# A selective scan with both directions' decay factors made in one instruction, one group ahead, and the matrix engine's queue reordered

## What is computed

```
dA  = exp(-delta[..., None] * exp(A_log))
dBu = delta[..., None] * Bm[:, :, None, :] * xc[..., None]
h   = dA * h + dBu          # for the five tokens in turn, h starts at 0
y   = einsum("bdn,bn->bd", h, c)
```

## Time and profile before

| | |
|---|---|
| Time, median of 3 runs | 537.95 us (536.87 to 539.11) |
| Time of the profiled execution | 537.0 us |
| Its span in the profile | 535.2 us |
| TensorE busy (matmul) | 484.4 us, 91% |
| VectorE busy | 380.0 us, 71% |
| ScalarE busy | 237.7 us, 44% |
| GpSimd busy | 171.3 us, 32% |
| The scan: first `argument` to last `outputs` | from 310.55 to 465.19 us of the span |

### The profile page before, as it was taken

How to read it: one execution, slowest core, us unless ns; L and a number is a source line. 1 busy time by engine, 2 the same in 40 slices (tenths; PEclk the granted TensorE clock), 3 DMA queues, 4 the chain that set the end, 5 groups by cost and what they waited for, 6 DMA issues and landing times. The chain is left out here.

```text
span 535.2 us, 6853 instructions
## 1 busy us (share of the span) xinstructions
PE 484.4 (91%) x1812; PEld 237.1 (44%) x1812; DVE 380.0 (71%) x718; ACT 237.7 (44%) x416; POOL 171.3 (32%) x163
## 2 busy tenths in 40 slices
PE   6989999999999998996879568989999998989997
PEld 3545555555555465543546312222222222376653
DVE  0066576575566677653999759999999999287655
ACT  1112213212222311659969537788878888121100
POOL 6000100100100112222250016888888888242000
PEclk9999999999999999999588959999999999999999
DMA  9981009300000000500334765665557565400000
GB/s 267 308 263 41 1 5 318 97 1 1 1 1 0 0 1 1 149 0 0 104 103 131 213 185 146 163 193 149 165 148 202 144 169 158 118 4 12 10 11 20
DMA packets 36426, 53.55 MB, mean 100 GB/s; under 512 B 5652, under 2 KB 27184, under 8 KB 36402
## 3 DMA queue, kind: packets, MB, share of 16 engines
q1 hardware_dynamic: 35746, 52.52, 34.3%
q10 hardware_dynamic: 656, 0.73, 0.4%
HBM read 35.83 MB, written 17.27 MB: 99 GB/s over the span
## 5 line engine op out<-in xcount | busy, mean ns | idle before, releaser
L1686 POOL TENSOR_TENSOR gb<-da,hb 128x512 f32<-128x512 f32 x94 | 117.1, 1281 | 65.8 <-ACT da L1622 65.8
L1716 DVE TENSOR_TENSOR da<-ps,expA 128x512 f32<-128x512 f32 x128 | 84.9, 683 | 10.1 <-PE ps L1520 8.9
L304 PE MATMUL ps<-xbuf,convw 128*128 128x384 f32 (+1 forms) x240 | 82.9, 499 | 4.8 <-DMA convw<-in_conv_wT 4.8
L1622 ACT ACTIVATE da<-da 128x512 f32<-128x512 f32 x128 | 78.0, 626 | 17.0 <-DVE da L1716 14.7
L358 PE MATMUL ps<-wall,peT 128*128 128x512 f32 x144 | 67.8, 593 | 0.0
L1520 PE MATMUL ps<-drows,selb 96*128 96x512 bf16 x128 | 50.5, 400 | 16.3 <-DMA drows<-dparts 10.5
L304 PEld LDWEIGHTS ps<-xbuf,convw 128*128 128x128 f32 (+1 forms) x240 | 46.0, 194 | 36.7 <-ACTq L501 4.0
L1532 PE MATMUL ps<-urows,brows 96*128 96x512 bf16 x128 | 48.8, 399 | 1.4 <-DVE gb L1723 0.8
L528 ACT ACTIVATE kvs<-ps 128x512 f32<-128x512 f32 x36 | 21.5, 597 | 57.4 <-PE ps L358 57.4
L520 ACT ACTIVATE peT<-ps 128x384 f32<-128x384 f32 x24 | 11.8, 491 | 75.4 <-PE ps L304 75.4
L1734 DVE TENSOR_TENSOR hb<-gb,ps 128x512 f32<-128x512 f32 x64 | 42.0, 676 | 0.0
(11 more groups left out here) (218 smaller groups left out, 746.4 us busy)
## 6 DMA issues: line engine op xcount, KB each, us to landing
xbuf<-in_xT SPq DMA_DIRECT2D x11, 768.0 KB
yscr<-yst SPq DMA_DIRECT2D x30, 208.0 KB
brows<-bparts SPq DMA_DIRECT2D x16, 240.0 KB, 3.3
uparts<-pt SPq DMA_DIRECT2D x24, 128.0 KB, 2.4
dparts<-pt SPq DMA_DIRECT2D x24, 128.0 KB, 2.4
drows<-dparts SPq DMA_DIRECT2D x15, 192.0 KB, 2.7
urows<-uparts SPq DMA_DIRECT2D x15, 192.0 KB, 3.2
inw<-in_in_wT SPq DMA_DIRECT2D x2, 1024.0 KB
```

The source lines that it names most:

```text
L304: mm = pe.matmul(bank(T_EMB + j % 2, 0, EN), convw[0:n, k, h * P:(h + 1) * P], xbuf[0:n, q, k, c * EN:(c + 1) * EN], start=(k == 0), stop= ...
L1622: act.activation(da_at(q, j), da_at(q, j), ACT.Exp, scale=-1.0).then_inc(da_ready, 1)
L1686: pool.tensor_tensor(gb_at(q, j), da_at(q, j), hb[:, s_ - 2, d, :], ALU.mult).then_inc({2: m2_done, 3: m3_done, 4: m4_done}[s_], 1)
L1716: dve.tensor_tensor(da_at(q, j), bank(j % 2), expA[:, j % 2, :], ALU.mult).then_inc(e_free, 1)
```

## The change

- `argument` and `exponential` become `arguments(g, q, s_)` and `exponentials(g, q, s_)`: one instruction of 128x1024 for both directions, four a group in place of eight of 128x512. `spread_delta` becomes `spread_pair`: two matmuls into banks 0 and 1, released together, and both banks are freed together.
- All four steps of group g+1 are made in the body of group g ("one group ahead"), and `spread_pair` of step 0 for group g+2 too. A new buffer `da1` holds steps 1 and 2 of odd groups.
- On TensorE, `spread_pair(g+1, 1)` stands ahead of `add_decayed(g-1, 1)` and `spread_pair(g+2, 0)` ahead of `add_decayed(g, 0)`.
- At the scan's start, VectorE makes the first decayed state and the first states of group 0 before it waits for the arguments of steps 2 and 3, whose rows arrive late. TensorE asks for the rows of group 1 before the first body.
- SyncE loads the delta rows of group g+2 at once, and the u and B rows behind the store of y.
- The expert weights `expw` move into the space of `inw`, which is no longer used by then, to make room for `da1`.

The number of matmuls, of states and of GpSimd instructions stays.

```diff
-        expw = sb("expw", [P, CH, E8 * C])
+        expw = inw[:, :, :, :].rearrange("p d h n -> p d (h n)")
+        da1 = sb("da1", [P, 4, DI], ctx=scn)
...
-        def da_at(q, j):
-            return da[:, j + (2 if j >= 6 and q == 1 else 0), :]
+        def da_at(q, j, n=1):
+            if j >= 2 and q == 1:
+                return da1[:, j - 2:j - 2 + n, :] if j < 6 else da[:, j + 2:j + 2 + n, :]
+            return da[:, j:j + n, :]
...
 # SyncE, body of group g
-                        sp.wait_ge(e_ready, 8 * g + 8)
-                        load_rows(sp, g + 2, q)
+                        sp.wait_ge(e_ready, 4 * g + 4)
+                        load_delta(sp, g + 2, q, 0, ST)
                     if last and q == 1:
                         last_y(0)
                     else:
                         store_y(g, 0)
+                    if not last:
+                        load_u(sp, g + 2, q, 0, ST)
+                        load_b(sp, g + 2, q)
...
 # TensorE
-            def spread_delta(g, q, j):
-                o = (j // 2) * DI
-                pe.wait_ge(e_free, 8 * g + j + 1)
-                pe.matmul(bank(j % 2), selb[:, j % 2, :], drows[:, q, o:o + DI],
-                          start=True, stop=True).then_inc(e_ready, 1)
+            def spread_pair(g, q, s_):
+                pe.wait_ge(e_free, 4 * g + s_ + 1)
+                for d in range(2):
+                    mm = pe.matmul(bank(d), selb[:, d, :], drows[:, q, s_ * DI:(s_ + 1) * DI], start=True, stop=True)
+                mm.then_inc(e_ready, 1)
...
             pe.wait_ge(d_landed[0], 16 * 2)
-            for j in range(4, 6):
-                spread_delta(0, 0, j)
+            spread_pair(0, 0, 2)
+            spread_pair(0, 0, 3)
+            pe.wait_ge(d_landed[1], 16)
+            spread_pair(1, 1, 0)
...
                     b_times_u(g, q, 4)
+                    b_times_u(g, q, 5)
+                    if after:
+                        spread_pair(g + 1, 1 - q, 1)
                     if not (first and q == 0):
                         add_decayed(g - 1, 1 - q, 1)
-                    b_times_u(g, q, 5)
-                    spread_delta(g, q, 6)
...
                     b_times_u(g, q, 6)
                     b_times_u(g, q, 7)
-                    spread_delta(g, q, 7)
                     if after:
-                        pe.wait_ge(d_landed[1 - q], 16 * (i + q) + (16 if q == 0 else 32))
-                        spread_delta(g + 1, 1 - q, 0)
+                        spread_pair(g + 1, 1 - q, 2)
                     outputs(g, q, 0)
...
                         b_times_u(g + 1, 1 - q, 0)
-                        spread_delta(g + 1, 1 - q, 1)
                         b_times_u(g + 1, 1 - q, 1)
-                        spread_delta(g + 1, 1 - q, 2)
-                        spread_delta(g + 1, 1 - q, 3)
+                        spread_pair(g + 1, 1 - q, 3)
                     if not (first and q == 0):
                         outputs(g - 1, 1 - q, 1)
                     if after:
-                        spread_delta(g + 1, 1 - q, 4)
                         b_times_u(g + 1, 1 - q, 2)
                         b_times_u(g + 1, 1 - q, 3)
+                    if not last:
+                        pe.wait_ge(d_landed[q], 16 * i + (48 if q == 0 else 32))
+                        spread_pair(g + 2, q, 0)
                     add_decayed(g, q, 0)
-                    if after:
-                        spread_delta(g + 1, 1 - q, 5)
...
 # ScalarE, body of group g
                         copy_state(g - 1, 1)
-                    exponential(g, q, 4)
-                    exponential(g, q, 5)
+                    if after:
+                        exponentials(g + 1, 1 - q, 0)
                     stage_c(g, q)
-                    exponential(g, q, 6)
-                    exponential(g, q, 7)
+                    if after:
+                        exponentials(g + 1, 1 - q, 1)
                     copy_y(g, 0)
...
 # VectorE
-            for j in range(3):
-                argument(0, 0, j)
-            decayed_1(0, 0, 0)
-            decayed_1(0, 0, 1)
-            argument(0, 0, 3)
+            for s_ in range(2):
+                arguments(0, 0, s_)
+            for d in range(2):
+                decayed_1(0, 0, d)
             for d in range(2):
                 state(0, 0, 1, d)
+            for s_ in range(2, 4):
+                arguments(0, 0, s_)
...
-                    argument(g, q, 4)
-                    argument(g, q, 5)
-                    argument(g, q, 6)
+                    if after:
+                        arguments(g + 1, 1 - q, 0)
                     state(g, q, 2, 0)
-                    argument(g, q, 7)
+                    if after:
+                        arguments(g + 1, 1 - q, 1)
                     state(g, q, 2, 1)
                     if after:
-                        for j in range(3):
-                            argument(g + 1, 1 - q, j)
-                        for d in range(2):
-                            decayed_1(g + 1, 1 - q, d)
-                        argument(g + 1, 1 - q, 3)
+                        arguments(g + 1, 1 - q, 2)
+                        decayed_1(g + 1, 1 - q, 0)
+                        decayed_1(g + 1, 1 - q, 1)
+                        arguments(g + 1, 1 - q, 3)
                         for d in range(2):
                             state(g + 1, 1 - q, 1, d)
```

More of the change, by code:

```diff
@@ L1242, in prepare_vector @@
             ch = Chain(dve, x_chain)
-            dve.sem_inc(e_free, 2)
+            dve.sem_inc(e_free, 1)
             dve.sem_inc(bu_used, 2)
@@ L1560, in scan_tensor @@
             pe.wait_ge(skip_ready, NI - 1)
-            for j in range(4):
-                spread_delta(0, 0, j)
+            for s_ in range(2):
+                spread_pair(0, 0, s_)
             pe.wait_ge(u_landed[0], 16 * 4)
@@ L1613, in scan_tensor @@
             pe.wait_ge(w_landed, W_ALL)
-            pe.wait_ge(e_free, 2 + 8 * NG)
+            pe.wait_ge(e_free, 1 + 4 * NG)
             keep_clock(6)
@@ L1619, in scan_scalar, with exponentials @@
         def scan_scalar(act):
-            def exponential(g, q, j):
-                act.wait_ge(e_free, 2 + 8 * g + j + 1)
-                act.activation(da_at(q, j), da_at(q, j), ACT.Exp, scale=-1.0).then_inc(da_ready, 1)
+            def exponentials(g, q, s_):
+                act.wait_ge(e_free, 1 + 4 * g + s_ + 1)
+                act.activation(da_at(q, 2 * s_, 2), da_at(q, 2 * s_, 2), ACT.Exp, scale=-1.0).then_inc(da_ready, 1)
             def copy_y(g, k):
@@ L1638, in copy_state @@
                 act.activation(hb[:, 2, d, :], bank(4 + d), ACT.Copy).then_inc(h3_copied, 1)
-            for j in range(4):
-                exponential(0, 0, j)
+            for s_ in range(4):
+                exponentials(0, 0, s_)
             def body(i, first, last):
@@ L1648, in body @@
                         copy_state(g - 1, 1)
-                    exponential(g, q, 4)
-                    exponential(g, q, 5)
+                    if after:
+                        exponentials(g + 1, 1 - q, 0)
                     stage_c(g, q)
-                    exponential(g, q, 6)
-                    exponential(g, q, 7)
+                    if after:
+                        exponentials(g + 1, 1 - q, 1)
                     copy_y(g, 0)
                     if after:
-                        for j in range(3):
-                            exponential(g + 1, 1 - q, j)
+                        exponentials(g + 1, 1 - q, 2)
+                        exponentials(g + 1, 1 - q, 3)
                     if not (first and q == 0):
@@ L1660, in body @@
                     if after:
-                        exponential(g + 1, 1 - q, 3)
                         copy_state(g, 0)
@@ L1674, in decayed @@
                 j = 2 * (s_ - 1) + d
-                pool.wait_ge(da_ready, 8 * g + j + 1)
+                pool.wait_ge(da_ready, 4 * g + s_)
                 if s_ == 4:
@@ L1685, in decayed @@
                     need(pool, y_done[1], g)
-                pool.tensor_tensor(gb_at(q, j), da_at(q, j), hb[:, s_ - 2, d, :],
+                pool.tensor_tensor(gb_at(q, j), da_at(q, j)[:, 0, :], hb[:, s_ - 2, d, :],
                                    ALU.mult).then_inc({2: m2_done, 3: m3_done, 4: m4_done}[s_], 1)
@@ L1706, in scan_vector, with arguments @@
             dve.wait_ge(skip_ready, NI)
-            def argument(g, q, j):
-                dve.wait_ge(e_ready, 8 * g + j + 1)
-                if j in (2, 3):
-                    need(dve, m2_done, 2 * g + j - 3)
-                elif j in (4, 5):
-                    need(dve, m3_done, 2 * g + j - 5)
-                elif j >= 6:
-                    need(dve, m4_done, 2 * g + j - 9)
-                dve.tensor_tensor(da_at(q, j), bank(j % 2), expA[:, j % 2, :], ALU.mult).then_inc(e_free, 1)
+            def arguments(g, q, s_):
+                dve.wait_ge(e_ready, 4 * g + s_ + 1)
+                if s_ == 0:
```

(11 more changed lines are left out.)

10 lines of the change are left out of this document (2 added, 8 removed).

## The result

The changed kernel takes 559.12 us (median of 4 runs, 558.02 to 561.70) against 537.78 us for the kernel before (4 runs): ratio 1.039, 95% interval 1.035 to 1.044. The forecast was 556.6 (543 to 566). The profiled execution has 558.86 us and a span of 557.1.

What follows compares the result with a forecast made beforehand. The prediction took VectorE as the bound in the scan of the kernel before. To the profiled 537.0 us it added 14.0 for the scan periods and 5.6 for the start, giving 556.6 us, range 543 to 566.

Steps and rivals of the forecast that it cites:

- The chain: Scan loop: waits through in-order queues from arguments to the next make periods 9.80 us, straight ones 9.58; +14.0 us, chance 0.63.
- The bound of +15.6 for a signal of 0.2: Scan periods: upper limit if the queue waits add up as summed, with 0.2 us for releasing TensorE; +15.6 us.
- The merging, 0.07 us a pair: VectorE arguments: one 1024-wide instruction starts its follower after 1.13 us against 1.20 for two; 0.28 us gained a group.
- The start: Scan start: late rows, both-bank hand-over and low TensorE clock delay group 1's first state; +5.6 us, +3.6 if the clock rises.
- The end: After group 15's first state: GpSimd's 7.45 us of work covers the arguments VectorE no longer has; 0 us.
- The DMA order: u and B rows, issued behind the store of y, land at 12.0 and are read at 15.6: hidden, 3 us to spare.
- The VectorE-bound case: Scan, faster rival: add_decayed and copy_state delay nothing, group takes 8.12 us, -9.1 us, total 531.5 us; chance 0.08.
- The period of 9.08 for bank waits only: Scan rival: outputs does not wait for stage_c, only waits before arguments 1 and 2 remain; +4.3 us, 545 to 546.5; chance 0.12.
- The clock did not fall in the loop: Scan rival: TensorE's clock falls inside the scan, +4.4 us a group affected, 565 for two, 579 for five; chance 0.11.

Runs made afterwards that it cites:

- Two edits that each cut one link: Changed kernel with add_decayed(g-1, 1) back ahead of the spreads of step 1: 548.7 us; or with stage_c ahead of the exponential: 551.2 us; both together: 550.5 us.
- the additions at the head in both kernels: Changed kernel with both add_decayed moved ahead of the spreads on TensorE: 537.7 us with 512-wide arguments, 544.9 us with 1024-wide ones.
- split kernels: Changed kernel with arguments 512 wide again, each bank filled and freed by itself: 550.8 us; with both add_decayed also ahead of the spreads: 537.7 us.
- the kernel with split arguments and early additions: Changed kernel with 512-wide arguments, single spreads and both add_decayed ahead of the spreads on TensorE: 537.7 us, ratio 0.999.
- the kernel with the addition back: Changed kernel with add_decayed(g-1, 1) back between the two b_times_u, ahead of the spreads of step 1: 548.7 us, ratio 1.020.

## Why the prediction was right

- **The chain, +14.0 forecast, +13.6 measured.** The links, forecast and measured from 376.15 on: arguments to spreads 1.31 and 1.28; spreads 0.43 and 0.44; addition to `copy_state` 1.06 and 1.06; `copy_state` to exponential 0.50 and 0.49; exponential to `stage_c` 0.95 and 0.95; `stage_c` to `outputs` 0.58 and 0.45 (0.59 in the other group of the pair); `outputs` to `b_times_u` 0.98 and 0.98; to `decayed_1` 0.51 and 0.42; and the rest of VectorE's queue 3.53 and 3.53. Two edits that each cut one link took 8.0 and 7.5 us away, and together 8.3: both links lie on one chain, shown. That the sum agrees to 0.4 us is in part luck: the 12 loop periods were 9.67 on average where 9.80 was forecast, 1.5 us less in all, and the two straight ones 10.67 and 9.61 in place of 9.58, 1.1 more, since the first of them still ran at the low clock. The bound of +15.6 for a signal of 0.2 should be +15.4 to +16.1 by the same terms.
- **The merging, 0.07 us a pair.** The row of SBUF to SBUF held for PSUM too: 1.13 to 1.14 from start to start, 1.22 long. The formula of the Trainium skill (VectorE: DVE Perf Modes, the section on the TRN2 errata) gives 1.224 us for the length, and the measured 1.22 agrees. What a queue gains by merging is the difference of start-to-start times. With the additions at the head in both kernels, merging lost 4.5 us in 14 periods.
- **The start, +5.6 forecast, +5.5 measured**, for the stated reasons. From the late rows' first spread (at 319.80, where the forecast has 317.31) the four arguments behind `arguments(0, 2)`, the `outputs` and the first state came after 3.43, 5.85, 8.20, 10.55, 10.45 and 15.36 us; 3.4, 5.8, 8.2, 10.6, 10.3 and 15.1 were forecast. The width is about 3 us of the start (split kernels 19.6 to 20.0 against 22.6); how the rest divides between the four more arguments and the clock is not shown. I had the clock low until group 1's first state; the changed kernel had 0.50 from 320 to 330, and 0.56 over the next ten.
- **The end, 0 forecast, 0.0 measured.** GpSimd's six products cover it. Neither of these two profiles has the slow row of the stage behind the scan, 1.7 us, that six others have; the sum had no term for it.
- **The DMA order**: hidden, as said; no wait of the scan in the loop ended on a transfer of rows.
- **The rivals.** The VectorE-bound case was the right mechanism for another order: it is what the kernel with split arguments and early additions does (8.45 a group). The period of 9.08 for bank waits only is near the 9.03 of the kernel with the addition back, in the sum and not in its terms: there, from start to start, 0.54 of wait lay before `arguments` of step 1 and 0.18 before step 2, where 0.31 and 0.65 were named. (Its time should be 545 to 547 by its own terms.) The clock did not fall in the loop.
- **The size.** 556.6 against a median of 559.1. The steps that I summed measured 19.1 us in the profile, and the medians lie 21.3 apart. The profiled execution lost 2.8 us ahead of the scan, for which the forecast had no term; whether any of this belongs to the change, four runs do not tell.

## What to carry to other kernels

In hand-ordered queues a merged instruction changes what waits behind it: follow each queue from the instruction that now ends later, on through every engine, until it comes back. A matmul that needs nothing new should not stand behind one that waits for the widest instruction of the loop; moving it, at no cost in work, was worth 8 us of 559. Two half-wide instructions on two banks, one filled while the other is read, can beat one wide instruction that frees both at once, here by 7.2 us.

## What the runs showed of the hardware that I had not expected

With eight extra matmuls of 0.86 us in front of the scan's start, TensorE's clock was up for the first spreads only (0.59 us a pair at 309.90, 1.03 at 317.76); with one or two more in each gap behind them it was 0.83 to 0.85 from 310 to 330, instead of 0.50. In the loop of the changed kernel TensorE was busy 14.55 of 18 us, with waits of 0.35 to 0.55 us several times a group, and the clock stayed at 1.00. The Trainium skill (TensorE: Matmul & The Clock Gate, the section on psum-queue depth-cycling) warns that cycling through PSUM banks can make the clock go to and fro; in this loop it did not. Behind the scan it fell in some profiles and not in others, with the same code there: 16 matmuls took 5.41 us in six of them and 3.72 in seven.
